# Attention scores from fp32 queries and keys in four groups of 32 partitions, in place of stacked bf16 parts

## What is computed

```python
q = einsum('oc,bct->bot', Wq, layernorm(x)) + bq      # 8 batches, 16 heads of 16 dims, 512 positions
k = einsum('oc,bcs->bos', Wk, ctx) + bk
v = einsum('oc,bcs->bos', Wv, ctx) + bv
dot = einsum('bhdt,bhds->bhts', q, k) / 4
mask = target_mask * source_mask
dot = mask * dot - (1 - mask) * 1e6
out = einsum('bhts,bhds->bhdt', softmax(dot) * mask, v)
x = x + out
x = x + moe(layernorm(x))                             # 8 experts, top 2 of softmax(x gate), silu(g) * u
```

## Time and profile before

| | |
|---|---|
| median of the runs | 974.7 us (970.87 to 975.07) |
| the profiled execution | 971.9 us, span 970.1 us |
| TensorE matmul busy | 820.0 us (85%) |
| VectorE busy | 547.9 us (56%) |
| GpSimd busy | 377.2 us (39%) |
| ScalarE busy | 316.5 us (33%) |
| DMA | 137.69 MB, 142 GB/s |
| granted TensorE clock, mean | 0.937 |

### The profile page before, as it was taken

The page is one execution under the profiler, slowest core; times in us unless marked ns, Lnnn a source line. Parts: engine busy times, 40 slices in busy tenths (PEclk is TensorE's granted clock), DMA queues, the critical chain, the costliest instruction groups (busy, mean ns, idle before and its releaser), DMA issues. The chain is left out here.

```text
span 970.1 us, 12844 instructions
## 1 busy us (share of the span) xinstructions
PE 820.0 (85%) x3737; PEld 366.6 (38%) x3738; DVE 547.9 (56%) x1055; ACT 316.5 (33%) x615; POOL 377.2 (39%) x396
## 2 busy tenths in 40 slices
PE   2078999999988998999899986159999999999994
PEld 1022323333333332333333322135555555555552
DVE  3186878788878877878788852403223232323322
ACT  0003556455545655555566675000000000000000
POOL 5643445457545754755474232401111111111111
PEclk9577999899999999999999998569999999999998
DMA  4553656566756856646664423322535365352332
GB/s 118 173 166 110 190 171 193 182 201 195 224 164 185 254 168 189 219 146 184 185 185 139 134 81 120 130 66 55 150 58 146 64 152 141 68 150 59 65 57 40
DMA packets 83567, 137.69 MB, mean 142 GB/s; under 512 B 13880, under 2 KB 39800, under 8 KB 83520
## 3 DMA queue, kind: packets, MB, share of 16 engines
q1 hardware_dynamic: 67792, 107.97, 36.7%
q0 software_dynamic: 7744, 17.86, 9.4%
q10 hardware_dynamic: 7984, 11.28, 4.0%
HBM read 77.34 MB, written 59.36 MB: 141 GB/s over the span
## 5 line engine op out<-in xcount | busy, mean ns | idle before, releaser
L731 DVE TENSOR_REDUCE mx<-tile 128x2 f32<-128x1024 f32 x256 | 309.0, 1217 | 67.8 <-PE tile L1005 64.8
L629 ACT ACTIVATE pr<-sc 128x512 f32<-128x512 f32 x512 | 268.8, 602 | 212.4 <-PE sc L992 209.5
L1005 PE MATMUL tile<-qk 97*128 97x512 bf16 x512 | 160.6, 397 | 43.8 <-DMA qk<-mrow_d 22.3
L1305 POOL DMA_INDIRECT out_dram<-y,ids x36 | 56.1, 1558 | 282.5 <-DVE ids L1230 278.4
L992 PE MATMUL sc<-qk 100*128 100x512 bf16 x512 | 156.2, 386 | 5.0 <-ACT pr L629 3.4
L1021 PE MATMUL pvb<-pr,vp 128*32 128x512 f32 x1024 | 141.3, 625 | 0.0
L1355 PE MATMUL dp<-wring,at 128*128 (+1 forms) x216 | 102.2, 609 | 13.4 <-DVE at L1240 13.4
L1285 ACT ACTIVATE sg<-gp 128x352 f32<-128x352 f32 x36 | 16.7, 463 | 291.7 <-PE up L1334 291.7
L1005 PEld LDWEIGHTS tile<-qk 97*128 97x128 bf16 x512 | 36.6, 98 | 182.5 <-DVE mx L731 75.9
L554 POOL TENSOR_SCALAR parts<-qkf 128x512 bf16<-128x512 f32 x32 | 48.3, 1511 | 140.5 <-DVE qkf L827 139.4
L1334 PE MATMUL gp<-wring,xtile 128*128 x288 | 94.0, 470 | 2.1 <-DVE meta L1221 2.1
(11 more groups left out here) (120 smaller groups left out, 742.2 us busy)
## 6 DMA issues: line engine op xcount, KB each, us to landing
qk<-stack_d SPq DMA_DIRECT2D x32, 768.0 KB
stack_d<-parts SPq DMA_DIRECT2D x32, 384.0 KB, 2.6
wring<-w_dram SPq DMA_DIRECT2D x32, 352.0 KB, 7.0
xl<-routed_d ACTq DMA_DIRECT2D x38, 257.0 KB, 2.7
stack_d<-parts SPq DMA_DIRECT2D x32, 256.0 KB, 2.9
pv_d<-ov SPq DMA_DIRECT2D x32, 256.0 KB, 3.5
xin<-x_dram SPq DMA_DIRECT2D x16, 256.0 KB, 5.8
cin<-ctxt_dram SPq DMA_DIRECT2D x8, 512.0 KB, 6.2
```

The costliest lines, as they stand in the source:

```text
L629: nc.scalar.activation(pr[s % 2][:, j, :], sc[(32 * u + 4 * s + j) % NSC][:, :], ACT.Exp, scale=SCALE).then_inc(exped.sem, 1)
L731: dve.tensor_reduce(mx[:, half(w), 2 * j:2 * j + 2], t[:, :, :], X, ALU.max, negate=True).then_inc(drained.sem, 1)
L1005: last = nc.tensor.matmul(t[:, i, :], qs[half(w)][0:RAW_ROWS, h, c * P:c * P + P], ks[half(w)][0:RAW_ROWS, h, :], start=True, stop=True)
L1305: pool.indirect_dma_start(out, bass.IndirectOffsetOnAxis(ap=ids[:, k, :], axis=0), y[:, k, :], None, compute_op=ALU.add).then_inc(y_added, 16)
```

## The change

Queries and keys stay fp32. A head has 16 rows of one group of 32 partitions, and a mask row and a maximum row beside them (18 rows in use); four heads j = 0 to 3 lie in the four groups of partitions, and two such sets g = 0, 1 beside each other in the free dimension. The weights' columns are reordered on the host to (group, dimension, set), so that a DMA from SBUF to SBUF moves 32 rows of `qkf` to 16 rows of `qk` (`move`). `qk` has three buffers in place of two. `part`, `keep_split`, `stack`, `split_maxima` and the DRAM tensor of the stack go. In a step, scores 2 and 3 are issued behind the second raw tile: scores 0 and 1 with raw scores of groups 2 and 3, product, raw scores of groups 0 and 1 with scores 2 and 3.

```diff
+GROUP = 32
+BIAS_ROW, MAX_ROW = D, D + 1
+RAW_ROWS, ALL_ROWS = D + 1, D + 2
+NQK = 3
+def raw_of(m):
+    return m // 8, m % 8 // 2, 2 - 2 * (m % 2)
...
-        qk = [sb(f"qk{i}", [P, 2, UH, T], BF16) for i in range(2)]
+        qk = [sb(f"qk{i}", [P, 2, 2, T]) for i in range(NQK)]
-        mx = sb("mx", [P, 2, 32])
-        mxt = sb("mxt", [96, P], BF16)
+        mx = sb("mx", [P, 2, 2, 4, 4])
+        mxt = sb("mxt", [32, P])
...
+            def move(u):
+                w = u + 2
+                sp.wait_ge(drained.sem, drained.at(u - 1, "k"))
+                if (due := scored.at(w - NQK, (7, 3))) is not None:
+                    sp.wait_ge(scored.sem, due)
+                dst = qk[w % NQK]
+                for j in range(4):
+                    at = GROUP * j
+                    sp.dma_start(dst[at:at + D, :, :, :], qkf[at:at + GROUP, half(w), :, :]).then_inc(moved.sem, 16)
+                sp.dma_start(dst[BIAS_ROW::GROUP, :, :, :],
+                             mrow_d[batch(w):batch(w) + 1].broadcast_to([4, 2, 2, T])).then_inc(moved.sem, 16)
...
             def unit(u):
-                if has(u + 1):
-                    stack(u + 1, 1)
+                if has(u + 2):
+                    move(u)
...
-                if has(u + 2):
-                    keep_split(u, 1)
...
-                if has(u + 2):
-                    sp.wait_ge(split_kept[0].sem, split_kept[0].at(u - 1, "k"))
-                    sp.wait_ge(split_kept[1].sem, split_kept[1].at(u, "k"))
-                    stack(u + 2, 0)
...
-                if has(u + 3):
-                    keep_split(u, 0)
...
-                    if (due := scored.at(u - 1, (7, 3))) is not None:
-                        sp.wait_ge(scored.sem, due)
-                    sp.dma_start(qs[half(w)][MAX_ROW:MAX_ROW + 3, :, :].rearrange("o h (c t) -> o (h c) t", t=P),
-                                 mxt[:, :]).then_inc(maxrows.sem, 16)
+                    sp.wait_ge(moved.sem, moved.at(u - 1, "m"))
+                    for g in range(2):
+                        sp.dma_start(qk[w % NQK][MAX_ROW::GROUP, g, 0, :], mxt[16 * g:16 * g + 16, :]
+                                     ).then_inc(maxrows.sem, 16)
...
         def _(pool):
+            for i in range(NQK):
+                pool.memset(qk[i][:, :, 1, :], 1.0).then_inc(ones_made, 1)
+                pool.wait_ge(ones_made, i + 1)
             for h in range(2):
-                pool.memset(ks[h][96:128, :, :], 1.0).then_inc(ones_made, 1)
...
             def scores(u, s, j):
-                nc.tensor.matmul(sc[(32 * u + 4 * s + j) % NSC][:, :],
-                                 ks[half(u)][0:ALL_ROWS, h, c * P:c * P + P],
-                                 qs[half(u)][0:ALL_ROWS, h, :], start=True, stop=True
-                                 ).then_inc(scored.sem, 1)
+                both = qk[u % NQK][GROUP * j:GROUP * j + ALL_ROWS, g, :, :]
+                nc.tensor.matmul(sc[(32 * u + 4 * s + j) % NSC][:, :], both[:, 1, c * P:c * P + P],
+                                 both[:, 0, :], start=True, stop=True).then_inc(scored.sem, 1)
...
             def raw_scores(u, m):
                 for i in range(2):
-                    h, c = (2 * m + i) // 4, (2 * m + i) % 4
-                    last = nc.tensor.matmul(t[:, i, :], qs[half(w)][0:RAW_ROWS, h, c * P:c * P + P],
-                                            ks[half(w)][0:RAW_ROWS, h, :], start=True, stop=True)
+                    at = GROUP * (first + i)
+                    both = qk[w % NQK][at:at + RAW_ROWS, g, :, :]
+                    last = nc.tensor.matmul(t[:, i, :], both[:, 0, c * P:c * P + P], both[:, 1, :],
+                                            start=True, stop=True)
...
             def transpose_maxima(u):
-                pe.wait_ge(maxsplit.sem, maxsplit.at(u, "p2"))
+                pe.wait_ge(drained.sem, drained.at(u, ("max", NPAIR - 1)))
...
             def unit(u):
                     for m in todo[:1]:
                         raw_scores(u, m)
-                    if has(u):
-                        scores(u, s, 2)
-                        scores(u, s, 3)
                     if s == 0 and has(u - 1):
                         product(u - 1, 7)
                     if s and has(u):
                         product(u, s - 1)
                     if s == 7:
                         ranks(u)
                     for m in todo[1:]:
                         raw_scores(u, m)
+                    if has(u):
+                        scores(u, s, 2)
+                        scores(u, s, 3)
```

More of the change, by code:

```diff
@@ L176, in build @@
         attention(nc, load_expert, x, ctxt, mask, maskc, maskd, wq, wk, wv, bq, bk, bv, gate, ident, ut, iotas,
[L177 removed]
+                  out, mrow_d, pv_d, recip_d, routed_d, idf, counts, io, tab, ends, pairi, pad)
         experts(nc, load_expert, wring, weights_in, out, routed_d, idf, tab, ends, pairi)
 def attention(nc, load_expert, x, ctxt, mask, maskc, maskd, wq, wk, wv, bq, bk, bv, gate, ident, ut, iotas,
[L182 removed]
+              out, mrow_d, pv_d, recip_d, routed_d, idf, counts, io, tab, ends, pairi, pad):
     st = ExitStack()
@@ L281, in attention @@
         normed = Count(sem("normed"), of(5, "n"))
-        split = [Count(sem(f"split{side}"), of(3 - side, 0, 1, 2, 3)) for side in range(2)]
-        split_kept = [Count(sem(f"split_kept{side}"), of(3 - side, "k"), 3 * 16) for side in range(2)]
-        stacked = [Count(sem(f"stacked{g}"), of(2 - g, "g"), 32) for g in range(2)]
+        moved = Count(sem("moved"), of(2, "m"), 5 * 16)
         vmade = Count(sem("vmade"), of(1, "v"))
-        maxsplit = Count(sem("maxsplit"), of(1, "p0", "r1", "p1", "p2"))
-        maxrows = Count(sem("maxrows"), of(1, "m"), 16)
+        maxrows = Count(sem("maxrows"), of(1, "m"), 32)
         den_in = Count(sem("den_in"), of(-1, "d"), 16)
@@ L461, in _ @@
             sp.wait_ge(const_made, MADE)
[L462 to L465, removed]
+            sp.wait_ge(ones_made, NQK + 2)
+            for g in range(2):
+                sp.dma_start(mrow_d[:, g], mrow[:, :, :]).then_inc(mrow_kept, 16)
             sp.wait_ge(mrow_kept, 32)
@@ L542, in token_rstd @@
                 pool.tensor_tensor(l2[:, 8:9], l2[:, 9:10], io[:, 1:2], ALU.pow).then_inc(rstd2.sem, 1)
[L544 to L563, removed]
             def residual(u):
@@ L589, in _ @@
                     batch_rstd(u)
-                if has(u + 3):
-                    part(u, 0)
                 if has(u - 1):
@@ L726, in maximum @@
                     return
-                if j == 0 and (due := maxsplit.at(u - 1, "r1")) is not None:
-                    dve.wait_ge(maxsplit.sem, due)
+                if j == 0 and (due := ready.at(u - 1, "maxT")) is not None:
+                    dve.wait_ge(ready.sem, due)
                 t = tile_of(u, ("max", j))
-                dve.tensor_reduce(mx[:, half(w), 2 * j:2 * j + 2], t[:, :, :], X, ALU.max, negate=True
+                g, c, first = raw_of(j)
+                dve.tensor_reduce(mx[:, half(w), g, first:first + 2, c], t[:, :, :], X, ALU.max, negate=True
                                   ).then_inc(drained.sem, 1)
[L734 to L752, removed]
-                    dve.tensor_tensor(mxp[:, 2, :], mxr[:, :], mxp[:, 1, :], ALU.subtract
-                                      ).then_inc(maxsplit.sem, 1)
             def maxima_out(u):
@@ L823, in projection_out @@
                 dve.wait_ge(ctx_in.sem, ctx_in.at(w - 3 - half(w), "c"))
-                if (due := split[side].at(u - 2 + side, 1)) is not None:
-                    dve.wait_ge(split[side].sem, due)
+                if (due := moved.at(w - 4, "m")) is not None:
+                    dve.wait_ge(moved.sem, due)
                 dve.scalar_tensor_tensor(
@@ L1391, with by_group @@
     iotas[:, 2] = -1.0
-    def by_dim(a):
-        return a.reshape(-1, 2, UH, D).transpose(0, 1, 3, 2).reshape(-1, C)
+    def by_group(a):
+        return a.reshape(-1, 2, 2, 4, D).transpose(0, 1, 3, 4, 2).reshape(-1, C)
     arrays = {
```

68 lines of the change are left out of this document (13 added, 55 removed).

## The result

The changed kernel takes 1139.8 us (median of four runs, 1133.5 to 1158.7) against 972.8 (median of four by now): 1.170 times the time before, 95% interval 1.163 to 1.177. That ratio leaves out the run of 1158.7 us, which fell into a slower state of the chip. The forecast was 1010 us, 968 to 1062: the sign was right, the size far off. The profiled execution took 1133.5 us.

What follows compares the result with a forecast made beforehand. The order and length of TensorE's work were taken to bound the attention. Turns +50 and start -14 gave +36 on the profiled 971.9, 1008; with the median 2.8 higher, 1010 us, range 968 to 1062.

Steps and rivals of the forecast that it cites:

- the clock falls: Rival: new waits of TensorE lower its clock, turns at half speed, beyond 1,200 us; chance 0.02.
- group G: Attention steps: four fp32 matmuls at once in four groups of partitions, taken as 1.05 us.
- score 1 behind the start of the second group: Next step's score 1 waits for score 2's exp: G + 0.75 us behind the second group's start.
- plain step: Step without an extra, product to product: 2G + 1.75 = 3.85 us, against 2.84 before.
- step with a projection: Step with a projection between the groups, which hides the exp wait: 4.92 us.
- step with values: Step with the values' matmuls between the groups, which hide the exp wait: 4.88 us.
- full turn: Turns 2 to 12: two plain steps, one with values, two with projections, three waiting for a slot: 36.0 us.
- turns, first to last score, beyond before: Attention turns: +39 us between first and last transposed maxima, +11 from there to the last score, together +50.
- start: Stretch until the first score: raw scores begin earlier without the wait for the stack; -14 us, bounds -4 and -19.
- Weight loads one by one: Rival: a group's weight loads go singly, G 1.19 to 1.35 us, total 1048 to 1090 us; chance 0.13.
- The four don't overlap: Rival: a group's four matmuls run one after another, G = 3.6 us, total about 1,650 us; chance 0.05.
- Faster: Rival: exps return in time and waits vanish, about 930 to 960 us, or 960 to 972 with waits halved; chance 0.12.

Runs made afterwards that it cites:

- the bf16 halves: The changed kernel with all 32 rows of each group named, reading only the upper 16 bits of queries and keys as bf16: 926.6 us, ratio 0.955.

## Why the prediction was wrong

**The step that failed** is the rival "the clock falls", to which the prediction gave a chance of 0.02, with the argument that waits of 1.5 us don't bring it down now; its sum holds no term for the clock in the turns. The argument looked for the cause in idle time only, while the change alters how many of the array's rows a matmul names, from 97 or 100 to four times 17 or 18. Instead the granted clock in the turns fell to 0.84, and the runs put 92.3 of the 163.6 us that the turns lost on this, measured by naming all 32 rows. Its size was wrong too: the rival said beyond 1,200 us, at half speed in all turns, and the clock was low for a third of the turns' time.

With all 32 rows named, and so without the low clock in the turns, the kernel takes 1038.3 us, inside the range and 28 above the forecast: I had the turns 21 too short and the start 9.

**Term by term**, against the kernel with 32 rows, where the clock is full:

| term | forecast | measured |
|---|---|---|
| group G | 1.05 | 1.07 (383.11 to 384.18 us) |
| score 1 behind the start of the second group | 1.80 | 1.88 |
| plain step | 3.85 | 3.92 |
| step with a projection | 4.92 | 5.05 |
| step with values | 4.88 | 5.12 |
| full turn | 36.0 | 37.1 |
| turns, first to last score, beyond before | +50 | +71 |
| start | -14 | -5 |

The mechanism in the turns was right: fp32 groups as long as the product, the exp of score 2 exposed in every plain step. Each size was short by 0.02 to 0.3 us. The largest part is at the extras, whose cost I had taken over from the kernel before: from the start of the extra to the next group it is 1.99 us for the values (1.78 before), 1.91 for a projection (1.82) and 0.99 for the logits (0.81). Why they cost more between groups wasn't tried. The eleven full turns take 410.3 us where I had 396 (eight of 37.1, the others 36.7, 38.1 and 38.7), 14 of the missing 21; the rest lies in the first two turns (+4) and the last ones.

**The start.** The first raw scores came at 31.2, as forecast, 15.8 earlier than before. But four raw tiles there take 7.54 us at the low clock, 1.9 each, where the bf16 row has two in 1.89. My +2 for this was too small by about 9: from first raw score to first score it now takes 48.4 us, before 37.2. The granted clock of the stretch is lower too, 0.58 (31 to 80 us) against 0.68 (47 to 84); how much is due to which wasn't taken apart.

**The rivals.** "Weight loads one by one" is out: all four first records start within 0.02 us. The page of the Trainium skill, TensorE: Matmul & The Clock Gate, section Part 3: Packing small matmuls, would have given G = 1.19 by its factor of 3.07, an estimate; measured is 1.07, that is 4 x 0.91 / 1.07 = 3.4 times, and the measurement decides. "The four don't overlap" is out. "Faster" would have needed results 0.7 us earlier; only the bf16 halves, which have that (first exp 0.47 behind the start of the group, 1.22 in fp32), are faster. The forecast of slower at 0.8 held.

**Off the path, as forecast:** GpSimd has 178 us less work and the DMAs 42 MB less traffic, and the steps at full clock show no gain from it; no run takes either alone. In the turns TensorE waits for no DMA, so `move` delayed nothing there.

## What to carry to other kernels

Before packing small matmuls, ask what it does to the clock, and not only to the time at full clock: look at the granted clock in the stretch, and if it dips while TensorE counts as busy, name all 32 rows of each group (zeros do) and run four groups at once; here that took the kernel from 1139.8 to 1038.3 us. Then look again where fewer matmuls run. And when matmuls get longer or closer together, follow one result through its reader to the matmul that reuses its bank: a chain of exp and signals that other matmuls had covered here cost 0.8 us a step once nothing stood in between.

## What the runs showed of the hardware

- These are single cases, no rule: with matmuls on 17 or 18 rows in each of four groups the granted clock in the turns was 0.84; on 32 rows of each, 1.00; with bf16 matmuls on 32 rows, one at a time, 0.72; on 97 or 100 rows, 0.98. TensorE was busy 92% or more of the stretch in all of these. Added rows of zeros did as well as added rows of ones. In the last turn, without raw scores, on 32 rows, it was 1.00 with three score banks (625 to 660 us) and 0.50 with two (646 to 691 us).
- Four fp32 matmuls of 512 columns in four row groups take 1.07 us from their start to that of the product, where one of full height takes 0.91; the first exp starts 1.22 us behind the group's start.
- A small VectorE instruction can last until the end of a GpSimd instruction of 1.3 us that runs beside it; whether it is a cast or an addition makes no difference.
